# Experts of a two-layer model: rows gathered by lists of tokens, results scattered in token order

## The reference, cut to what matters

```python
x = x + L0_attn(layernorm(x), ...)   # complex gated recurrence, group norm, dense feed-forward
x = x + L0_ffn(layernorm(x), gate_kernel, w0, w1, wo)      # 64 experts, two per token
x = x + L1_attn(layernorm(x), ...)   # state space scan (16 states, 512 channels)
x = x + L1_ffn(layernorm(x), w_router, gate_up_proj, down_proj, w_gate, w_up, w_down)  # 16 experts, one per token
```

## Time and profile before

| | |
|---|---|
| median of 3 runs | 3593.39 us (3588.81 to 3599.57) |
| the profiled execution | 3591.36 us |
| its span, first to last instruction | 3589.6 us |
| mean granted clock of TensorE | 0.846 of full speed |
| busy: TensorE / DVE / ScalarE / GpSimd | 73% / 59% / 29% / 34% |
| moved by the DMA engines | 426.74 MB, 119 GB/s over the span |

### The profile page before, as it was taken

One profiled execution on the slowest core, in us unless ns is written; L12 is line 12 of the kernel. 1 busy time (PEld: TensorE's weight loads), 2 busy tenths in 40 slices (PEclk: granted clock), 3 DMA queues, 4 the chain that ended last, 5 costly groups with the idle time before them and its releaser, 6 DMA issues. The chain is left out here.

```text
span 3589.6 us, 38815 instructions
## 1 busy us (share of the span) xinstructions
PE 2618.9 (73%) x11942; PEld 1793.3 (50%) x11942; DVE 2105.9 (59%) x3889; ACT 1044.9 (29%) x1613; POOL 1234.1 (34%) x689
## 2 busy tenths in 40 slices
PE   5655299761599999994266777767778668956993
PEld 2222166561499999994022332333323325636993
DVE  8999778364121112213698998998989963231221
ACT  4444122100111111111345545455455322101110
POOL 1222144305100000003658678687686740021003
PEclk8767699955799999997578988888889888978996
DMA  4110100001699999995200000000101000007995
GB/s 161 64 64 32 40 12 18 12 1 66 215 333 330 332 331 332 332 334 175 71 24 24 36 24 36 24 35 24 36 24 36 35 18 0 0 31 258 330 332 173
DMA packets 299023, 426.74 MB, mean 119 GB/s; under 512 B 23728, under 2 KB 197168, under 8 KB 294848
## 3 DMA queue, kind: packets, MB, share of 16 engines
q1 hardware_dynamic: 264384, 377.58, 31.4%
q0 software_dynamic: 9216, 25.18, 2.2%
q10 hardware_dynamic: 25344, 23.08, 1.9%
HBM read 362.58 MB, written 63.18 MB: 119 GB/s over the span
## 5 line engine op out<-in xcount | busy, mean ns | idle before, releaser
L1283 POOL TENSOR_TENSOR ss_h<-ss_h,ss_cs 128x2048 f32<-128x2048 f32 x128 | 579.0, 4525 | 89.7 <-DVE ss_h L1609 81.7
L1353 PE MATMUL ss_y<-ss_h,all_ident 128*128 128x512 f32 x1024 | 534.0, 671 | 27.9 <-POOL ss_h L1283 27.8
L1068 DVE TENSOR_TENSOR experts_in<-experts_sil,experts_pU 128x512 f32<-128x512 f32 x176 | 121.1, 688 | 665.4 <-PE experts_pU L1005 665.4
L1609 DVE TENSOR_TENSOR_SCAN ss_h<-ss_da,ss_c_h,ss_dbu 128x512 f32<-128x512 f32 x384 | 470.7, 1268 | 46.6 <-ACT ss_da L1479 40.7
L1353 PEld LDWEIGHTS ss_y<-ss_h,all_ident 128*128 128x128 f32 x1024 | 222.1, 220 | 314.7 <-issue 278.4
L1479 ACT ACTIVATE ss_da<-ss_dt,ss_decay 128x512 f32<-128x512 f32 x512 | 326.5, 711 | 178.2 <-POOL ss_dt L1259 90.7
L1005 PE MATMUL experts_pG<-experts_xt,experts_wg 128*128 128x128 f32 x2816 | 346.6, 277 | 0.0
L1005 PE MATMUL experts_pU<-experts_xt,experts_wu 128*128 128x128 f32 x2816 | 344.4, 276 | 0.0
L1014 PE MATMUL experts_pY<-experts_wd,experts_in 128*128 128x256 f32 x1408 | 332.7, 379 | 0.0
L1005 PEld LDWEIGHTS experts_pG<-experts_xt,experts_wg 128*128 128x128 f32 x2816 | 331.8, 193 | 0.1
L1602 DVE TENSOR_TENSOR ss_dbu<-ss_dtx,ss_bB 128x1024 f32<-128x1024 f32 x256 | 314.4, 1228 | 28.9 <-PE ss_bB L1345 1.2
(11 more groups left out here) (298 smaller groups left out, 3886.4 us busy)
## 6 DMA issues: line engine op xcount, KB each, us to landing
experts_wg<-in_w SPq DMA_DIRECT2D x128, 512.0 KB, 4.3
experts_wu<-in_w SPq DMA_DIRECT2D x128, 512.0 KB, 5.6
experts_wd<-in_wo SPq DMA_DIRECT2D x128, 512.0 KB, 6.7
ss_cs<-ss_c_rows SPq DMA_DIRECT2D x32, 1024.0 KB, 4.6
experts_wg<-in_gate_up SPq DMA_DIRECT2D x48, 512.0 KB, 4.7
experts_wu<-in_gate_up SPq DMA_DIRECT2D x48, 512.0 KB, 5.9
experts_wd<-in_down SPq DMA_DIRECT2D x48, 512.0 KB, 7.1
experts_xr<-moe_xs SPq DMA_DIRECT2D x176, 128.0 KB, 3.8
```

The costliest lines, as they stand in the source:

```text
L1068: nc.vector.tensor_tensor(IN[t.two][:].rearrange("p f t -> p (f t)"), SIL[t.two][:], pU[t.two][:], ALU.mult)\
L1283: pool.tensor_tensor(h[:], h[:], CS[q % 2][:, n % GROUP].unsqueeze(1).to_broadcast([P, CI, BT]), ALU.mult)\
L1353: mm = pe.matmul(y[:, c], ident[:], H[n % RING][:, c], start=(n == 0), stop=(n == N - 1))
L1609: ins = V.tensor_tensor_scan(H[n % RING][:, c], DA[n % 2][:, c], DBU[:, c % 2], first, ALU.mult, ALU.add)
```

## The change

In words: the second pass of `route` is gone. Instead of rows, the first pass sends, per token and choice, an entry of 8 bytes (the token's number, and its place `token * K + k` in token order) to a list of its expert in HBM. Each expert's list has room for all 4096 tokens, so a slot is known from expert and rank alone and does not wait for the counts. `gate_loop` fills the lists with blank entries (a token number of a row of zeros, a place outside the result) where it filled the arrays with zeros, and GpSimd waits for these DMAs before its loop. The normalised rows are written once, in token order, by SyncE (`r.rows`; for the second experts weighted, with the row of `X` beside them, 2 KB in all). At the end of `route` one indirect gather reads the lists of all tiles, and a transpose makes `r.token` and `r.place`.

`expert_tiles` gathers each tile's rows by token with an indirect DMA on GpSimd and scatters its results by place with another; SyncE issues only weights and ScalarE no stores. Results of the first experts thus lie in token order and `state_space` reads them with 8 direct loads of 1 MB into 8 buffers (the scan's state, C and decay buffers); places outside the result are not written. In the second, `X` is added as the result is copied out of PSUM, and the scatter writes the output itself: `combine` is gone.

In `state_space` the order of DVE changes with it, block 0's small steps move from GpSimd to DVE (`first_steps`), and exponential and logarithm of the next block become two calls, at states 9 and 10.

The diff, cut to its core:

```diff
 # gate_loop, SyncE and GpSimd
-                def fill(i):
-                    for array in to_zero:
...
-                        sp.dma_start(part, zeros[:].unsqueeze(1).to_broadcast([P, n, D])).then_inc(s["zeroed"], 16)
...
+                for r, empty in zip(routes, blank):
+                    lists = r.lists.rearrange("(a p) w -> p a w", p=P)
+                    sp.dma_start(lists, empty.rearrange("p s w -> p (s w)").unsqueeze(1).to_broadcast(list(lists.shape)))\
+                        .then_inc(s["zeroed"], 16)
...
+                pool.wait_ge(s["zeroed"], 32 * len(routes))
                 with pool.Fori(0, NB) as i:
 # route, SyncE
+                for b in range(NB):
+                    sp.wait_ge(s["xw_done" if shared else "xn_done"], (b + 1) * TPB)
+                    sp.dma_start(rows[b, :, :, 0:D], XN[b % 2][:]).then_inc(rows_stored[b % 2], 16)
+                    if shared:
+                        sp.wait_ge(s["shared_added"], b + 2)
+                        sp.dma_start(rows[b, :, :, D:2 * D], X[:, b * TPB:(b + 1) * TPB]).then_inc(s["x_stored"], 16)
 # route, GpSimd
-                            for k in range(K):
-                                pool.indirect_dma_start(r.xs, bass.IndirectOffsetOnAxis(ap=SL[h][:, j, k:k + 1], axis=0),
-                                                        XS[h][:, j], None).then_inc(sent[h], 16)
+                for b in range(NB):
+                    pool.wait_ge(s["slots_ready"], b + 1)
+                    for j in range(TPB):
+                        for k in range(K):
+                            pool.indirect_dma_start(lists, bass.IndirectOffsetOnAxis(ap=SL[b % 2][:, j, k:k + 1], axis=0),
+                                                    entry[:, b * TPB + j, k], None).then_inc(listed[b % 2], 16)
                 for h in range(2):
+                    pool.wait_ge(listed[h], LISTED * (NB // 2))
+                pool.wait_ge(s["list_done"], 1)
+                pool.indirect_dma_start(LST[:].rearrange("p s w -> p (s w)"), None, r.lists,
+                                        bass.IndirectOffsetOnAxis(ap=LIST_I[:], axis=0)).then_inc(s["fetched"], 16)
 # route, DVE
+                def place(b):
...
+                    V.scalar_tensor_tensor(SL[b % 2][:], IDX[:], float(T), RK[:], ALU.mult, ALU.add).then_inc(s["slots_ready"], 1)
...
+                for b in range(NB):
+                    choose(b)
...
+                    elif b < NB - 2:
+                        normalise(b + 2)
+                    place(b)
                     if shared:
+                        weigh(b)
...
+                for w in range(2):
+                    V.tensor_copy(LF[:, w], LST[:, :, w]).then_inc(s["split_done"], 1)
+                dve.wait_ge(s["list_turned"], 1)
+                V.tensor_copy(r.token[:], pR[:, 0:P])
+                V.tensor_copy(r.place[:], pR[:, P:2 * P]).then_inc(s["list_done"], 1)
 # expert_tiles
-                    sp.dma_start(XR[t.b][:], xs[bass.ds(t.t, 1)].rearrange("t p d -> (t p) d")).then_inc(x_loaded[t.b], 16)
...
+                def gather(t):
+                    if t >= BUF:
+                        pool.wait_ge(s["xt_raw"], t - BUF + 1)
+                        pool.wait_ge(s["y_done"], t - BUF + 1)
+                    pool.indirect_dma_start(XR[t % BUF][:], None, r.rows, bass.IndirectOffsetOnAxis(ap=r.token[:, t:t + 1], axis=0))\
+                        .then_inc(x_loaded[t % BUF], 16)
+
+                def scatter(t):
+                    pool.wait_ge(s["y_done"], t + 1)
+                    to = bass.IndirectOffsetOnAxis(ap=r.place[:, t:t + 1], axis=0)
+                    pool.indirect_dma_start(r.ys, to, Y[t % BUF][:], None, bounds_check=T * r.K - 1, oob_is_err=False)\
+                        .then_inc(stored[t % BUF], 16)
+
+                for t in range(AHEAD):
+                    gather(t)
+                for t in range(N):
+                    if t + AHEAD < N:
+                        gather(t + AHEAD)
+                    scatter(t)
...
-                def store(t):
-                    act.wait_ge(s["y_done"], t.t + 1)
-                    act.dma_start(ys[bass.ds(t.t, 1)].rearrange("t p d -> (t p) d"), Y[t.b][:]).then_inc(stored[t.b], 16)
...
+                    if r.direct:
+                        nc.vector.tensor_tensor(Y[t.b][:], XR[t.b][:, D:2 * D], pY[t.two][:, 0:D], ALU.add).then_inc(s["y_done"], 1)
 # state_space
+                def fetch(b):
+                    sp.dma_start(Y[b].rearrange("p j k d -> p j (k d)"), rows[b]).then_inc(fetched[b], 16)
...
+                def first_steps():
+                    ch = Chain(dve, s["tail"])
+                    for half in range(2):
...
+                        ch.link(V.tensor_scalar(REST, e, 1.0, 1.0, ALU.add, ALU.subtract))
+                        ch.link(V.tensor_tensor(REST, e, REST, ALU.subtract))
+                        ch.link(V.tensor_tensor(u, u, REST, ALU.add))
+                    for half in range(2):
...
+                        V.tensor_tensor(u, u, LN1[:, part], ALU.add).then_inc(s["dt_done"], 1)
+                        wait(dve, "dt_done", half + 1)
+                        V.tensor_tensor(DTX[0][:, part], u, XC[0][:, part], ALU.mult).then_inc(s["dtx_done"], 1)
...
                 add_experts(0)
                 row_stats(0, 1)
...
                 add_experts(1)
+                add_experts(2)
                 for c in range(CI):
                     convolve(0, c)
-                add_experts(2)
+                    add_experts(c + 3)
+                add_experts(NB - 1)
                 split_bc(0)
-                add_experts(3)
-                row_stats(1, NB // 2 - 1)
+                row_stats(1, NB - 1)
+                first_steps()
...
+                        if prep and n == 9:
+                            exponential(b + 1)
                         if prep and n == 10:
-                            exp_log(b + 1)
+                            logarithm(b + 1)
 # build
-        combine(nc, "combine1", X, r1, out=out)
```

More of the change, by code:

```diff
@@ L140, in gate_loop @@
         zeros = m_.sb("zeros", [P, D])
+        blank = [T3[:, n, 0:2 * P].bitcast(I32).rearrange("p (s w) -> p s w", w=2) for n in range(len(routes))]
         quarter = m_.sb("quarter", [P, 1])
@@ L676, in route, with wait @@
         s = {n: m_.sem(n) for n in names}
-        sent = [m_.sem(f"sent{h}") for h in range(2)]
-        SENT = 16 * TPB * K
+        listed, rows_stored = ([m_.sem(f"{n}{h}") for h in range(2)] for n in ("listed", "rows_stored"))
+        LISTED = 16 * TPB * K
         LOADED = 16 * (4 if shared else 1)
-        def blocks(engine, body):
-            with engine.Fori(0, NB // 2 - 1) as q:
-                body(q * 2, 0, True)
-                body(q * 2 + 1, 1, True)
-            body(NB - 2, 0, True)
-            body(NB - 1, 1, False)
+        def wait(engine, name, value):
+            if value > 0:
+                engine.wait_ge(s[name], value)
         with nc.Block() as block:
@@ L879, in body @@
[L879 to L886 removed]
+                        x = X[:, b * TPB:(b + 1) * TPB]
+                        V.tensor_tensor(x, x, pS, ALU.add).then_inc(s["shared_added"], 1)
+                        if b < NB - 2:
+                            normalise(b + 2)
                 ch.link(V.tensor_scalar(NTILE[:], COUNT[:], 1.0 / P, 0.5 - 0.5 / P, ALU.mult, ALU.add))
@@ L926, in _ @@
-                send(0, False)
-                with dve.Fori(1, NB // 2) as i:
-                    send(i, True)
-                dve.wait_ge(s["owner_turned"], 1)
-                V.tensor_copy(r.expert[:], pL[0:1, 0:P]).then_inc(s["expert_ready"], 1)
+                if not shared:
+                    dve.wait_ge(s["exp_done"], 1)
+                    ch.link(V.tensor_scalar(DEN[:], EX[:], 1.0, None, ALU.add))
+                    ch.link(V.reciprocal(W0[:], DEN[:]))
+                    ch.mark(V.tensor_scalar(r.weight[:, :, 0], W0[:], 1.0, None, ALU.mult))
+                    ch.mark(V.tensor_tensor(r.weight[:, :, 1], W0[:], EX[:], ALU.mult))
@@ L988, in _ @@
                 steps(sp, load)
+            @block.gpsimd
+            def _(pool):
+                def gather(t):
[15 more added lines that the diff above has]
+                    scatter(t)
+                for b in range(BUF):
+                    pool.wait_ge(stored[b], 16 * (N // BUF))
             @block.tensor
@@ L1198, in _ @@
                         .then_inc(s["loaded"], 16)
+                for b in range(1, NB):
+                    fetch(b)
                 def store_rows(b):
@@ L1490, in _ @@
                     copy_dt(0, c)
-                exp_log(0)
+                exponential(0)
+                logarithm(0)
+                wait(act, "added", (RING + 3) * TPB)
                 decays(0, 0)
@@ L1503, in _ @@
                             copy_bc(b + 1)
+                        if b == 0 and n == 0:
+                            wait(act, "added", NB * TPB)
                         if n < N - 1:
```

375 lines of the change are left out of this document (145 added, 230 removed).

## The result

The changed kernel takes 3686.37 us, median of 4 runs (3675.98 to 3697.22), beside 3593.63 us of the kernel before (3588.81 to 3599.57): a ratio of 1.0265, 95% interval 1.0246 to 1.0285. It is slower by 2.6%; the forecast was 3538 us, 1.5% faster. The time lies inside the forecast's wide range (3400 to 3700), at its upper end, but on the other side of the kernel before.

What follows compares the result with a forecast made beforehand. The expert stages were taken as bound by TensorE with the DMA engines nearly full. From 3591.4 us, gains of 222 (82 + 44 + 41 + 55) and a loss of 169 gave 3538 us, 1.5% less; range 3400 to 3700.

Steps and rivals of the forecast that it cites:

- the loss of 169 us: Expert stages: TensorE stalls on gathered rows, 0.90 us for 124 tiles (112) and 1.30 for 44 (57).
- so 2.97: Expert stages: gathered rows land 2.97 us after the gather instruction, as beside a 2 MB load; 1.87 with idle DMA engines.
- rival B: Expert stages: gather waits for weights issued before it (period 8.0, 3789 us) or clock falls each step (3669); chance 0.31.
- the weights have landed by about S + 7.8: Expert stages, S the step's start: nothing then delays the gather, so landing ends by 8.0, not S + 8.7.
- rival A: Expert stages: chain stays within 5.52 us, loads land as on idle engines, only gains left, 3369 us; chance 0.17.
- the next step begins when it ends: Expert stages: the chain closes on itself within one step, so its 6.42 us (6.82 in the second) is the period.
- The clock, left at full: Expert stages: stalls of 0.9 us in 6.4 keep the full clock; if it fell, the loss would be 300.
- 1 us more: Last combining stage: it goes, 56.2 us, leaving a last scatter 1 us longer than today's store; gain 55.
- First router: Second pass goes, list scatters run beside ranking: 79 us less after the pass, 3 within; gain 82 (70 to 88).
- rival C: Routers: lists are late because 8-byte rows cost GpSimd more, say twice, 2.2 us; 3593 us; chance 0.05.
- Second router: Of 57.4 us between the windows, chain 2, gather 3.5, casts and transposes 2, border 6 remain; gain 44 (28 to 46).
- Preparation: Combining after first experts and scan preparation: direct loads, earlier normalise, first steps on DVE; gain 41 (30 to 46).

Runs made afterwards that it cites:

- the changed kernel once more: The changed kernel, unaltered, timed and profiled again beside the kernel before: 3664.94 us, ratio 1.0199.
- rows first: Changed kernel, with SyncE asking for a tile's weights only after a small GpSimd instruction behind that tile's gather: 3502.58 us, ratio 0.9764.

## Why the prediction was wrong

**The links of the chain were right, one term and its closing were not.** The changed loop is bound by result, scatter, gather, landing, transposes, as forecast: TensorE's idle time ends with the DMA of rows, and taking the gather off the chain gives 5.5 us back at once. The sign was wrong because the loss of 169 us was 299.

**The term that failed: the landing, "so 2.97".** I took the gather of the earlier trace rows beside a load as "the same kind of traffic". It measured 4.48 us (5.12 in the second stage, where I allowed 0.4 for the bytes). I read that row as having 2 MB beside it, but the two loads of it were asked for at 1744.11 and 1744.49, 5.3 and 5.0 us before the gather (1749.44), and the first had landed at 1749.04. What the row did not have is 1.5 MB asked for 1.8 us ahead; the experiments give 2.6 without it, 4.5 with it, 2.9 with it asked for behind. In the changed kernel once more the last weight load lands 4.15 us after the gather's end and the rows 4.43 us after it, in the median: they come in just behind the weights. This is rival B's first mechanism, in a size between its "period 8.0" and my row. The 5.3 us of the stores was the better row: I used it as an upper end and then argued it away with "the weights have landed by about S + 7.8". The rule of the Trainium skill that I weighed (DMA: Bandwidth & Descriptors, Queues, rings and completion order: an engine takes turns between its queues) would have given rival A; the trace is against it here as far as a landing can tell, 4.48 us behind the weights and 2.89 ahead of them. It is no strict order of asking either: in the kernel with the gather ahead of the scatter the last weight load is asked for 0.6 us after the gather began, while its descriptors are still written, and lands 5.99 us after the gather's end, behind the rows (4.96).

**The step that failed in the other direction: "the next step begins when it ends".** I had the result copied 0.62 us after the transposes of the next tile, as it is when TensorE never waits. Once it waits, the result is copied before those transposes, at the end of its own step, and the chain spans two steps. With the measured 5.82 us and otherwise my own prices that is (5.82 + 0.42 + 0.60 + 0.97 + 0.30 + 0.96 + 2.97) / 2 = 6.02 us, not 6.42; in the second stage 6.22, not 6.82. The loss would have been 0.50 x 124 + 0.70 x 44 = 93 us and the forecast 3462. The error shortened the distance to the truth by 76 us: two mistakes of opposite sign, and the larger one won.

Put together, starting from these 93 us: the landing (1.51 and 1.75 us more, halved) adds 94 and 38, which makes 225, about as much as the gains. So the landing alone takes away the whole win; that the kernel is slower, and not equal, comes from the smaller terms below: some 23 us in the other links of the chain, 16 of the clock in the second stage, 21 at the edges of the stages. That is 285 of the 299. Rival B's price by the clock, 3669, is near the measured time by luck: the clock of the first stage was 0.98.

**The smaller terms of the chain.** The wait before the scatter was 0.81 us, my upper end, not 0.60; the scatter took 1.02, not 0.97.

**The clock, left at full.** In the first stage it was close to it (0.98). In the second it was 0.90, and the interval of 7.59 is 0.35 above the chain's (5.82 + 2.57 + 0.97 + 5.12) / 2 = 7.24: about 16 us. Windows of TensorE in the second stage of the kernel after, cut at the transposes (length, busy, granted clock, DMA):

```profile
3448.20:3457.20 9.00, 5.66 (x44) 1.00 0.74 239
3457.20:3464.40 7.20, 7.20 (x43) 0.76 0.65 236
...
3464.40:3473.40 9.00, 5.69 (x44) 0.94 0.77 240
3473.40:3481.70 8.30, 8.30 (x43) 0.66 0.58 205
```

A step that ends in 3.3 us of waiting is followed by one without any wait that takes 7.2 or 8.3 us for the same matmuls, at a mean clock of 0.76 and 0.66, so part of it at the lower level of 1.2 GHz. The stalls are not spread evenly over the tiles as I had them: here they fall on every other step and take 3.3 us, where the stalls of over 1 us in the first stage take 2.1 in the median and its clock stays at 0.98. My reading of the earlier trace rows was off too: I put the idle time of 3.89 us into the second window, but it ends at 2181.41 in the kernel before:

```profile
2181.41 0.59 PE L1345 MATMUL ss_bB<-ss_bc,ss_sel 128*128 128x512 bf16 x1 [3.89 <-DVE ss_dbu L1602]
```

So 2.5 us of it lie in the first window, whose clock is 1.00; the low clock is in the window in which the idle time ends.

**The edges of the expert stages: "1 us more".** With eight buffers nothing waits inside the stages (5.55 and 5.60 us), and they are still 11.4 and 12.1 us longer than before, 23.5 us that the sum did not have. The first gather goes out at 865.85 and the first transposes are at 872.39, 6.5 us; at the other end, in the kernel after:

```profile
1773.99 0.98 POOL L1011 DMA_INDIRECT moe_ys<-experts_y,moe_place  x1 [0.74 <-DVE experts_y L1087]
1781.80 0.11 POOL L1197 MEMSET ss_sel<- 128x16 bf16 x1 [6.83 <-POOLq L109]
```

6.8 us from the last scatter to the next stage, on the path. Before, the first transposes came 2.0 us after the first load of rows (933.89 and 935.90), and the next stage 3.9 us after the copy of the last result had ended (1653.19 to 1657.10); here it is 8.6 us (1773.21 to 1781.80).

**The gains held.** First router: 68 in the first profile (just below the range), 86 in the second and 85.5 with eight buffers, forecast 82 (70 to 88). The pass itself runs at 10.5 us a block where nothing outside holds it up, against my 10.8, and the list scatters are 1.26 us apart with 8 bytes a row as with 1 KB: rival C is out. Second router 53.0, forecast 44, above its range (46): after the last block's sum 9.8 us remain (3276.1 to 3285.9) where I had 13, and the pass takes 236.6 us, 242 before, which I had at no gain. Preparation 39.3 (41), with the first scan 100.4 us after the start of its stage (99). Last combining 56.2 (55). Scan loop -2.0 in one profile and +1.4 in the other (0). With the chain gone the kernel has a span of 3379.3 us, where rival A had 3369.

## What to carry to other kernels

When a load is moved behind a result, draw the loop in its stalled state, count how many steps it spans, and take its landing from a row in which the same large transfers are asked for just ahead of it, not from one with the same total traffic. Before moving such a load, give it the buffers that take it off the result: here eight small buffers instead of four (1 or 2 KB a partition each) turned 2.0 to 2.6% slower into 6.0% faster with the same loads, gathers and products. Where buffers are short, the order of asking is worth nearly as much as bytes: rows first gave back 162 of the 286 us (3502.58 us), and loading 640 KB of 1536 KB came to 3465.16 us.

## What the hardware showed that I had not expected

- A small gather asked for 1.8 us after 1.5 MB of direct loads on another queue landed in 4.48 us after its end; asked for ahead of them, in 2.89. 640 KB in front cost it 0.3 us over all gathers.
- An increment of a semaphore placed behind an indirect DMA on GpSimd is not ordered behind its issue: the loads that waited for it went out 0.15 us before the DMA began. A MEMSET with the increment, placed there, ran when the gather had ended (1410.23), and the loads went out 1.0 us later.
- The indirect DMA's time on GpSimd did not depend on its payload: 0.96 us at 8 bytes a row, 0.97 for the gathers of 1 KB and 2 KB rows.
- Waits on an unnamed releaser held the first router up by 18 us in one profile and not in the next of the same program.
